# Two transformer layers on one core: the mixtures' front joined into one block, the expert rows combined in the experts' block, the next attention's norms per tile, and its context prepared in the first prelude

## The reference

```python
x = x + _L0_xattn_ref(_layernorm(x), ctx, ctx, ...)      # 16 heads of 16, relative positions
x = x + _L0_ffn_ref(_layernorm(x), ...)                  # 8 experts, top 2, inner width 512 (gate and up: 1024)
x = x + _L1_xattn_ref(ctx, _layernorm(x), mask, ...)     # 16 heads of 64, keys: 1024 latents and 77 context rows
x = x + _L1_ffn_ref(_layernorm(x), ...)                  # 8 experts, top 2, inner width 1024, capacity 1024
```

```python
xn = layernorm(x, ln_x_g, ln_x_b)          # x is the context here
ln = layernorm(latents, ln_l_g, ln_l_b)    # latents is _layernorm(x) of the residual
kv = jnp.concatenate([xn @ Wkv, ln @ Wkv], axis=1)
sim = jnp.where(padded_mask[:, None, None, :], sim, max_neg)
```

```python
out = ye[idx1, pos1] * (w1 * keep1)[:, None] + ye[idx2, pos2] * (w2 * keep2)[:, None]
```

## Time and profile before

| | us |
|---|---|
| median of 3 runs | 2371.99 |
| lowest and highest run | 2366.87, 2379.66 |
| profiled execution, its own time | 2374.06 |
| its span, first to last instruction | 2372.3 |
| TensorE busy | 1998.0 (84%) |
| VectorE busy | 1255.8 (53%) |
| ScalarE busy | 908.9 (38%) |
| GpSimd busy | 621.2 (26%) |

### The profile page before, as it was taken

The page is one execution under the profiler, slowest core; times in us unless marked ns, Lnnn a source line. Parts: engine busy times, 40 slices in busy tenths (PEclk is TensorE's granted clock), DMA queues, the critical chain, the costliest instruction groups (busy, mean ns, idle before and its releaser), DMA issues. The chain is left out here.

```text
span 2372.3 us, 37776 instructions
## 1 busy us (share of the span) xinstructions
PE 1998.0 (84%) x12252; PEld 1542.5 (65%) x12253; DVE 1255.8 (53%) x3015; ACT 908.9 (38%) x1746; POOL 621.2 (26%) x570
## 2 busy tenths in 40 slices
PE   5788648999048999999999999999999824999993
PEld 3568535666037887787788888778787613676762
DVE  4371145666435667666677666766667615112223
ACT  3543212222024555454555555555555401222320
POOL 2200002332145324332343332433224001222220
PEclk9999858999557999999999999999999965999997
DMA  4412261111303122112221112211222064101113
GB/s 180 158 42 99 110 229 53 46 46 40 101 17 78 46 64 64 37 44 49 63 56 45 46 46 64 64 44 39 47 63 57 1 254 158 32 32 33 33 31 117
DMA packets 93669, 167.59 MB, mean 71 GB/s; under 512 B 22129, under 2 KB 54575, under 8 KB 91451
## 3 DMA queue, kind: packets, MB, share of 16 engines
q1 hardware_dynamic: 82875, 142.65, 20.8%
q0 software_dynamic: 8320, 20.65, 3.0%
q10 hardware_dynamic: 2304, 2.10, 0.3%
HBM read 79.90 MB, written 32.41 MB: 47 GB/s over the span
## 5 line engine op out<-in xcount | busy, mean ns | idle before, releaser
L1661 DVE TENSOR_REDUCE a_part_peak<-a_slot 128x1 f32<-128x512 f32 (+1 forms) x512 | 354.6, 731 | 316.2 <-PE a_slot L1486 315.7
L1623 ACT ACTIVATE a_probT<-a_slot 128x640 f32<-128x640 f32 x256 | 180.4, 705 | 483.1 <-PE a_slot L1495 261.7
L1486 PE MATMUL a_slot<-a_KHL,a_QHL 128*128 128x512 f32 (+1 forms) x1536 | 343.7, 359 | 20.9 <-DVE a_probT L1684 10.2
L1486 PEld LDWEIGHTS a_slot<-a_KHL,a_QHL 128*128 128x128 f32 x1536 | 271.8, 190 | 120.1 <-issue 52.7
L1611 ACT ACTIVATE a_prob<-a_slot,a_npeak 128x1024 f32<-128x1024 f32 x256 | 284.2, 1110 | 3.9 <-DVE a_npeak L1663 3.9
L1511 PE MATMUL a_po<-a_probT,a_V 128*64 128x256 f32 (+1 forms) x2304 | 277.0, 385 | 0.0
L1495 PE MATMUL a_slot<-ident,a_prob 128*128 128x128 f32 x2048 | 268.9, 275 | 0.0
L1495 PEld LDWEIGHTS a_slot<-ident,a_prob 128*128 128x128 f32 x2048 | 237.8, 144 | 8.5 <-issue 0.2
L1438 PE MATMUL a_side<-a_W,a_latT 128*128 128x128 f32 x1536 | 205.0, 286 | 22.3 <-DVE a_KT L1671 10.4
L1511 PEld LDWEIGHTS a_po<-a_probT,a_V 128*64 128x64 f32 (+1 forms) x2304 | 153.6, 136 | 87.3 <-issue 21.8
L1438 PEld LDWEIGHTS a_side<-a_W,a_latT 128*128 128x128 f32 x1536 | 191.4, 200 | 28.3 <-DVE a_KT L1671 14.9
(11 more groups left out here) (320 smaller groups left out, 3028.1 us busy)
## 6 DMA issues: line engine op xcount, KB each, us to landing
a_KHL<-a_KT SPq DMA_DIRECT2D x128, 256.0 KB, 4.3
a_QHL<-a_QT SPq DMA_DIRECT2D x128, 128.0 KB, 2.3
m_up<-_L_ffn_gate_up_proj_dram SPq DMA_DIRECT2D x8, 1024.0 KB
m_up<-in_L_ffn_W_dram SPq DMA_DIRECT2D x8, 1024.0 KB
m_down<-in_L_ffn_W_dram SPq DMA_DIRECT2D x8, 1024.0 KB
a_prob_dram<-a0p_zeros SPq DMA_DIRECT2D x4, 1632.0 KB, 10.6
a_dist_dram<-a_dist SPq DMA_DIRECT2D x4, 1632.0 KB, 8.2
a_band_prob<-a_prob_dram SPq DMA_DIRECT2D x4, 1632.0 KB, 6.8
```

What stands on the lines that cost most here:

```text
L1486: ins = t_.matmul(out[:, lo:hi], q, KHL[:, pair.parity, h, part, lo:hi], start=part == 0, stop=part == 1)
L1623: a_.activation(probT[:, u // 4 % 2, HALF:KT_TILES, h, u % 2 * P:(u % 2 + 1) * P], slot[u % 2][:, HALF * P:KT_TILES * P].rearrange("p (t q ...
L1661: v.tensor_reduce(part[:, i:i + 1], slot[u % 2][:, lo:hi], AX.X, ALU.max).then_inc(part_peaked, 1)
```

## The change

Three parts.

1. `front` takes the place of the load block, `layer_norm` and `route`: one block. SyncE issues the constants, six up projections, the row stores as tiles become ready, then the other two up projections, the up bias and the down projections whose place is free, and waits for the stores. TensorE turns tile t and then takes the logits of tile t - 2. In mixture 0 the transposes are written to `a1_latT`, the next attention's tile, so only four down projections' places are lent; in mixture 1 four as well. The lent down projections and the down bias are now loaded in the experts' block (`load_rest`), and the wait for weights is split: up at step 0, down at step 2.
2. `experts` gets `follow`: the combination runs in the experts' own block. In layer 1 it is `Combine`, the same code as before. In layer 0 it is `Bridge`: SyncE loads the next attention's first pair weights and then, after the last scatter, the result rows; VectorE adds each tile, takes its statistics at once and normalises the tile four before it; the two norms are one, with the variance v taken to v (1 + eps) + eps^2 before the power; TensorE turns, ScalarE writes `latT`, and GpSimd does the six context operations.
3. `ContextPrelude`: the context's loads, norm and transposes move into the second block of layer 0's prelude. Its loads are issued after the zeros; VectorE's statistics stand between the two halves of the `kblock` products.

```diff
+class ContextPrelude:
...
+    def sync(self, sp):
+        C, I = self.C, self.I
+        for dst, src in ((C.lng, "ln_l_g"), (C.lnb, "ln_l_b"), (self.cng, "ln_x_g"), (self.cnb, "ln_x_b")):
+            sp.dma_start(dst[:, :], I[f"L1_xattn_{src}"]).then_inc(self.loaded, 16)
+        sp.dma_start(self.qg[:, :], I["L1_xattn_qn_g"]).then_inc(self.loaded, 16)
+        sp.dma_start(self.kg[:, :], I["L1_xattn_kn_g"]).then_inc(self.loaded, 16)
+        sp.dma_start(self.mask[:, :, :].rearrange("p b k -> p (b k)"),
+                     I["mask"].to_broadcast([P, BATCH * CTX])).then_inc(self.loaded, 16)
+        sp.dma_start(self.maskT[:, :], I["maskT"]).then_inc(self.loaded, 16)
+        sp.dma_start(self.c[:, :, :], I["ctx"].rearrange("b k e -> k b e")).then_inc(self.loaded, 16)
...
+    def statistics(self, dve):
+        s, v, C = Steps(dve, self.step), self.nc.vector, self.C
+        dve.wait_ge(self.loaded, 144)
+        s.mark(v.tensor_copy(C.maskf[:, :, :], self.mask[:, :, :]))
+        s.mark(v.tensor_scalar(C.maskn[:, :, :], self.mask[:, :, :], -1.0, 1.0, ALU.mult, ALU.add))
+        s.mark(v.tensor_copy(C.valid[:, :], self.maskT[:, :]))
+        s.mark(v.scalar_tensor_tensor(C.gamma[:, :], self.qg[:, :], D1 ** 0.5, self.kg[:, :], ALU.mult, ALU.mult))
+        for b in range(BATCH):
+            s.after(v.bn_stats(self.stats[:, b, :], self.c[:, b, :]))
+            s.after(v.bn_aggr(self.moments[:, b, :], self.stats[:, b, :]))
+        v.tensor_scalar(self.var[:, :], self.moments[:, :, 1], LN_EPS, None, ALU.add).then_inc(self.var_done, 1)
+
...
                     sp.dma_start(prob_d[n].rearrange("p j h -> p (j h)"), zeros[:, :]).then_inc(cleared, 16)
+                context.sync(sp)
                 sp.wait_ge(cleared, 16 * NN)
...
                                 mask[:, :].unsqueeze(2).to_broadcast([P, GROUP, CTX]), ALU.mult)
+                    if far == 0:
+                        context.statistics(dve)
+                context.normalise(dve)
...
-            refill(sp, logits_done, inverse_done)
+            load_constants(sp)
+            load_weights(sp, 0)
+            for t in range(TILES):
+                sp.wait_ge(dst_done, t + 1)
+                sp.dma_start(xn_rows[t * P:(t + 1) * P, :], xn[:, t, :]).then_inc(rows_stored, 16)
+            load_weights(sp, 1)
...
+            def logits_of(t):
+
+                pe.wait_ge(copied, t + 1)
                 for c in range(EC):
                     ins = nc.tensor.matmul(pl[:, t, :], xnT[:, c, t * P:(t + 1) * P], Wr[:, c, :],
                                            start=c == 0, stop=c == EC - 1)
-            ins.then_inc(logits_done, 1)
+                return ins
+
+            for t in range(TILES):
+                pe.wait_ge(dst_done, t + 1)
+                if t >= 4:
+                    pe.wait_ge(copied, t - 3)
+                for c in range(EC):
+                    ins = nc.tensor.transpose(turned[t % 4][:, c, :], xn[:, t, c * P:(c + 1) * P], ident[:, :])
+                ins.then_inc(turned_done, 1)
+                if t == 2:
+                    pe.wait_ge(*constants_loaded)
+                if t >= 2:
+                    logits_of(t - 2)
+            logits_of(TILES - 2)
+            logits_of(TILES - 1).then_inc(logits_done, 1)
             pe.wait_ge(masks_done, 1)
             m = M[:, :, :].rearrange("p s e -> p (s e)")
             nc.tensor.matmul(pp[:, 0, :], before[:, :], m, start=True, stop=True)
@@ -711,12 +835,36 @@
 
         @block.scalar
...
-                    pe.wait_ge(weights_ready[0], weights_ready[1])
+                    pe.wait_ge(*up_ready)
+                if isinstance(s, int) and s == 2:
+                    pe.wait_ge(*down_ready)
...
+class Combine:
...
+    def sync(self, sp, scattered):
+        sp.wait_ge(scattered, 16 * BLOCKS)
+        for t in range(TILES):
+            if t >= 4:
+                sp.wait_ge(self.added, t - 3)
+            sp.dma_start(self.got[t % 4], self.rows[t]).then_inc(self.loaded[t % 4], 16)
...
+class Bridge(Combine):
...
+    def sync(self, sp, scattered):
+        for i in range(2):
+            sp.dma_start(self.W[:, i].rearrange("p i c n -> p (i c n)"),
+                         self.I["L1_xattn_Wpair"][i:i + 1].rearrange("a p i c n -> p (a i c n)")).then_inc(self.w_loaded[i], 16)
+        super().sync(sp, scattered)
...
+        pool.wait_ge(self.copied, TILES // BATCH + 1)
...
+        for t in range(TILES):
+            self.add(dve, t)
+            dve.wait_ge(self.added, t + 1)
+            v.bn_stats(self.stats[:, t, :], self.xres[:, t, :]).then_inc(self.stats_done, 1)
+            if t >= LN_GROUP:
+                normalise(t - LN_GROUP)
+            dve.wait_ge(self.stats_done, t + 1)
+            v.bn_aggr(self.moments[:, t, :], self.stats[:, t, :]).then_inc(self.moments_done, 1)
+            if t % LN_GROUP == LN_GROUP - 1:
+                dve.wait_ge(self.moments_done, t + 1)
+                cols = slice(t + 1 - LN_GROUP, t + 1)
+                v.tensor_scalar(self.variance[:, cols], self.moments[:, cols, 1], 1.0 + LN_EPS, LN_EPS * LN_EPS,
+                                ALU.mult, ALU.add).then_inc(self.variance_done, 1)
+        for t in range(TILES - LN_GROUP, TILES):
+            normalise(t)
+
...
+            def load_weights(sp, stage):
+
+                for e in range(NE - 2) if stage == 0 else range(NE - 2, NE):
+                    sp.dma_start(up[:, e], I[wup][e].rearrange("(c p) n -> p c n", p=P)).then_inc(up_loaded, 16)
+                if stage == 1:
                     sp.dma_start(bup[:, :, :].rearrange("p e n -> p (e n)"),
-                                 I[wbup].to_broadcast([P, NE * E * 4])).then_inc(weights_loaded, 16)
-                    load_down(sp, range(NE - 2 * lent))
-            layer_norm(nc, f"{name}ln", xres, xn, ident, xnT, store=(xn_rows, rows_stored))
-            route(nc, f"{name}r", layer, xnT, lists, (Wr, br, iota, lane, before), (constants_loaded, 16 * len(constants)), refill)
+                                 I[wbup].to_broadcast([P, NE * E * 4])).then_inc(up_loaded, 16)
+                    load_down(sp, range(NE - lent))
+
+            def load_rest(sp):
```

More of the change, by code:

```diff
@@ L648, in route @@
         Wr, br, iota, lane, before = constants
+        stats = sb("stats", [P, TILES, 6])
+        moments = sb("moments", [P, TILES, 2])
+        variance = sb("variance", [P, TILES])
+        exponent = sb("exponent", [P, TILES])
+        rstd = sb("rstd", [P, TILES])
+        turned = [ctx.enter_context(nc.psum_tensor(f"{name}_turned{i}", [P, EC, P], F32)) for i in range(4)]
+        stats_done, moments_done, variance_done = sem("stats_done"), sem("moments_done"), sem("variance_done")
+        exponent_set, rstd_done, dst_done = sem("exponent_set"), sem("rstd_done"), sem("dst_done")
+        turned_done, copied = sem("turned_done"), sem("copied")
         ones = sb("ones", [P, P])
@@ L719, in _, with moments_of @@
         def _(dve):
+            def moments_of(g):
+                tiles = range(g * LN_GROUP, (g + 1) * LN_GROUP)
+                for t in tiles:
+                    nc.vector.bn_stats(stats[:, t, :], xres[:, t, :]).then_inc(stats_done, 1)
+                for t in tiles:
+                    dve.wait_ge(stats_done, t + 1)
+                    nc.vector.bn_aggr(moments[:, t, :], stats[:, t, :]).then_inc(moments_done, 1)
+                dve.wait_ge(moments_done, tiles.stop)
+                cols = slice(tiles.start, tiles.stop)
+                nc.vector.tensor_scalar(variance[:, cols], moments[:, cols, 1], LN_EPS, None, ALU.add).then_inc(variance_done, 1)
+            moments_of(0)
+            for g in range(TILES // LN_GROUP):
+                if (g + 1) * LN_GROUP < TILES:
+                    moments_of(g + 1)
+                dve.wait_ge(rstd_done, g + 1)
+                for t in range(g * LN_GROUP, (g + 1) * LN_GROUP):
+                    nc.vector.tensor_scalar(xn[:, t, :], xres[:, t, :], moments[:, t, 0:1], rstd[:, t:t + 1],
+                                            ALU.subtract, ALU.mult).then_inc(dst_done, 1)
             s = Steps(dve, step)
@@ L868, in within, with _ @@
             return not isinstance(b, int) or 0 <= b < BLOCKS
+        @block.sync
+        def _(sp):
+            load_rest(sp)
+            after.sync(sp, scattered)
         @block.gpsimd
@@ L1034, in mixture, with __init__, scalar, tensor @@
-def mixture(nc, I, xres, ident, layer, out=None):
+            after.vector(dve)
+class Combine:
+    def __init__(self, nc, ctx, name, gates, y_rows, xres, h, out):
+        self.nc, self.gates, self.xres, self.out = nc, gates, xres, out
+        self.got = [h[:, i // 2, i % 2 * TOPK * E:(i % 2 + 1) * TOPK * E].rearrange("p (k e) -> p k e", k=TOPK) for i in range(4)]
+        self.loaded = [nc.alloc_semaphore(f"{name}_loaded{i}") for i in range(4)]
+        self.added, self.half = nc.alloc_semaphore(f"{name}_added"), nc.alloc_semaphore(f"{name}_half")
```

(36 more changed lines are left out.)

316 lines of the change are left out of this document (152 added, 164 removed).

## The result

The kernel after takes 2273.81 us, the median of 4 runs (2266.02 to 2280.04), against 2372.26 us (2366.87 to 2379.66) before: a ratio of 0.9581, 95% interval 0.9542 to 0.9621. The forecast was 2268 us, in a range of 2248 to 2292, so the measured median lies 5.8 us above it.

The account below looks back on a forecast made before the run. Hand-overs between stages, where TensorE idles behind DMA issues and serial small work, were taken as the bound; terms summed to -104.1 us, from 2374.06 to 2270.0 profiled, median 2268 us, range 2248 to 2292.

Parts of the forecast that it names:

- Fronts: Start of both mixtures: norm starts with the weight issue, logits are read earlier, -28.4 us in mixture 0, -42.0 in mixture 1.
- Rival 3: Gain smaller than counted: TensorE's clock rises in the joined fronts (2257 us) or the context is hidden (2248 us); chance 0.12.
- Gathers and down loads: Start of the experts' blocks: step 2 waits for down weights, gathers share the DMA engines; +1 us mixture 0, +2 mixture 1.
- if the first gather takes over 5 us: Sign of being wrong, at the start of the experts' blocks: the first gather takes over 5 us.
- rival 1: Experts' blocks: gathers land only when the loads issued with them have, +13 us mixture 1, +7 mixture 0: 2288 us; chance 0.12.
- Bridge: Mixture 0 to attention 1: combination and next norm in the experts' tail bring attention 1's first product earlier, -38.8 us.
- Leaving the block 1.6 us: End of mixture 0's experts' block: 1.6 us from the tail's end at 640.1 to attention 1's start at 641.7.
- rival 2: Experts' tails: the 7.3 us of leaving belong to the block's end and come back, 5.7 us more, twice: 2279 us; chance 0.10.
- Context: First prelude: context loads queue behind 6.5 MB of zeros and land at about 53 us, +9.4 us, bounds 0 and 12.4.
- Attention 0 and 1: The two attention stages: no change counted, 0 us for each.
- the prediction's last sign: Sign of being wrong, in attention 1: its loop changes its length.
- end: End of mixture 1: the additions start without the 7.3 us of leaving the block, -7.3 us.

Follow-up runs that it names:

- the first run: The kernel after, unchanged, measured once more: median 2266.98 us, ratio 0.9573 against the kernel before.

## Why the prediction was right, point by point

**Fronts.** Right in mechanism. The norm starts with the first issue in both mixtures, and the logits are read 23.4 us later where the sum had 25.7 and 25.4. Rival 3's rising clock did not come: the granted clock stays at 0.50, the 1.2 GHz level, through the interleaved part (the windows above). The term was built from 21.2 us of TensorE work at the low clock. A tile measured 1.17 us, not 1.33: a tile's four router products took 0.72 us between transpositions, less than the 0.86 that a sixteenth of the earlier trace rows's 13.79 us gives. The order of issue was rightly held to be hidden, as the run with the weights first shows. Nor did SyncE end a front late: from the logits to the first gather it is 28.3 and 29.6 us, 28.2 and 29.3 before. What the change gained here is almost all the barrier; the interleaving has 1.0 us a front.

**Gathers and down loads.** The forecast put +1 and +2 on a wait at step 2 and on the gathers. The wait did not come; +3.5 and +3.9 us came on the gathers, and with 6.4 and 6.8 us one of the prediction's own signs of being wrong, "if the first gather takes over 5 us", came true. The step that failed is the row that it took as nearest, the gather at 2013.36 of the kernel before, "beside 1 MB of bias". It was beside nothing. The windows of the kernel before show that the bias had moved when that gather's data began to:

```profile
2013.00:2014.00 1.00, 0.00 (x0) 0.00 (x0) 0.00 (x0) 0.00 (x0) 0.64 (x1) 0.61 0.96 393
2014.00:2015.00 1.00, 0.00 (x0) 0.00 (x0) 0.00 (x0) 0.00 (x0) 0.69 (x2) 0.50 0.07 25
2015.00:2016.00 1.00, 0.00 (x0) 0.00 (x0) 0.00 (x0) 0.00 (x0) 0.70 (x1) 0.50 0.45 131
```

Its 2.94 us are those of a gather alone, and holding the loads back gave the same (2.90 to 2.97 us). In the kernel after a backlog stands beside it, 5 MB in mixture 1 and in mixture 0 the 3 MB counted and 0.75 MB of pair weights, which `Bridge` issues right behind them and the prediction left out. So the mechanism is rival 1's, in part: the gathers wait 3.9 us of its 14 and 3.5 of its 8, not for the whole of the loads. The Trainium skill ("DMA: Bandwidth & Descriptors", "Queues, rings and completion order") has the engines round-robin between queues at packet granularity. The trace agrees that a gather overtakes the loads (in mixture 0 it is read at 353.94, and the DMA engines still move 375 GB/s at 358 to 359), but it waits 3.5 to 3.9 us beside them, not a few packets' time, and the measurement decides. What makes it that long is not shown.

**Bridge.** Rows 2.4 us after the scatter, 33.8 us of chain against 34.4: right. The step that failed is "Leaving the block 1.6 us": it is 6.4, and rival 2 named why, that the 7.3 us belong to the block's end and not to the fresh scatter. Shown by two runs: the time counts from GpSimd's last instruction, and an early drain takes it away. A second step failed with it, that GpSimd's six context operations are hidden: they end 3.0 us after the power that they stand behind, and the run with them ahead of it is 2.3 us shorter. Rival 2's "twice" was wrong: mixture 1 ends with the program, and its rows are asked for 2.42 us after the scatter's issue with nothing given back (3.1 us from last addition to the end, 3.0 before). And of the 34.6 us gained the norms per tile are 11.7; the rows asked for earlier are 7.4 (9.78 us before, 2.41 now), the weights loaded ahead 3.7 (37.1 less 33.4), and the rest, 11.8, is the context's prelude that no longer stands there: from first addition to first norm it was 30.4 us before and is 18.6 in the run with own norms. The 11.7 has the slow exit inside it; without it the norms per tile would be worth the 17 us told there.

**Context.** +10.5 against +9.4, with the reason given (loads behind the zeros); they landed at 54.2 us, where the sum had 53. The issues took 1.25 us each, not 0.47, behind a full queue, and the power 3.2 us.

**Attention 0 and 1.** The sum held them fixed. Attention 0 is 13 us uncertain between executions of the same code, and this one term moved the profiled span more than any misjudged one. The terms of the sum miss in both directions (fronts -2.4 and -2.0, gathers +2.5 and +1.9, Bridge +4.2, prelude +1.1, end -0.7), so that the stages it counts gave 99.6 us in the profile of the kernel after and 98.7 in the first run's, not 104.1. That the first run's median, 2266.98 us, is within 1.1 us of the forecast is therefore partly luck: both attentions were faster there than in the profile of before, by 1.8 and 6.1 us. Attention 1 is 3.5 us shorter in the kernel after, so the prediction's last sign, a loop that changes its length, is neither met nor excluded by twelve profiles in which it ranges over 8 us.

What stays open: why the granted clock of attention 0 falls for some 25 us in one execution and not in another, and whether attention 1's 1224 to 1233 us in the twelve profiles and 1236.1 in that of before is more than that.

## What to carry to other kernels

A block that only issues DMAs ends with its last issue, and before a full queue that can be 26 us; put such issues into a block where another engine works anyway, and count nine small loads as 4 us if they stand alone. When GpSimd has issued indirect DMAs in a block whose last stage ends on other engines, give GpSimd's part and its drain an earlier place: its exit counts from its own last instruction. A small transfer is priced beside a backlog only by a row in which the backlog is still moving. Traffic moved off a barrier comes back where the next block's first small transfer starts; hold it until that one has landed, and wait for it where it is first read.

## What the runs showed of the hardware that was not expected

- GpSimd takes some 5 to 6.5 us to drain after a run of indirect DMAs, also if the last landed 35 us earlier; a second drain is cheap (GpSimd's last instruction to its next one 2.59 us with the early drain, 7.74 without). In a block without indirect DMAs it was 2.15 us.
- A stall of 8.8 us costs TensorE more than its length: the next eight products took 6.27 us instead of 3.69, at a granted clock of 0.50 for their first 4 us.
- 64 router products of 8 columns, back to back, did not keep the clock up: behind dense transpositions it rose to 1.00 and was back at 0.50 some 4 us later, with TensorE busy 2.00 us of every 2.
- An indirect gather of 128 rows took 2.9 us from issue to reader alone, 6.4 and 6.8 us beside 3.75 and 5 MB on SyncE's queue.
- SyncE's issue of a small load took 0.43 us with an empty queue and 1.25 us behind 6.5 MB of zeros.
- GpSimd's power of 77x2 values took 3.23 us beside VectorE's four products of two operands (2.92 us), 0.72 us alone.
- The same attention took 220.6 to 233.6 us in twelve profiles; in two of them the granted clock of one 30 us stretch was 0.60 and 0.94.
